# Even steps: the 128-wide rest of the slot is issued after the step's half bulk operation

## The chip, the core and the metric

One core of a Trainium2 chip runs the whole program. The metric is the device time of one execution in microseconds (us), the median of several runs. One execution was also recorded by the hardware profiler.

## What is computed

The input x is 8 sequences of 2048 tokens with 512 features, in fp32. Cut to what matters:

```python
xn = layernorm(x)
x_norm = layernorm(xn, g, b); x_norm += conv3(x_norm)            # depthwise, 3 taps
gate, input_gate = split(x_norm @ gate_w.T + gate_b)
Bm = x_norm * sigmoid(input_gate) @ B_w.T + B_b                  # 64 wide
Cm = x_norm @ C_w.T + C_b
def step(state, (b_t, c_t)):                                     # 2048 of these, in sequence
    s = layernorm(state @ A_bar + b_t, g_st, b_st)
    return s, c_t * s
s = (scan(step) @ D_w.T + D_b) * sigmoid(gate)
out = x + s * silu(xn @ W.T + b + (xn @ V_r) @ C.T)
```

The scan is the only part that is sequential over time. Its state is 8 sequences by 64 numbers.

## The kernel before

The 2048 tokens are cut into 32 chunks (NC) of 64 tokens (CT). All engines run the same loop over chunks, called `iteration(i, ...)`. In iteration i the scan (part F) goes through chunk i, while the dense work of part A prepares chunk i+1 and that of part C finishes chunk i-1. Nothing is planned by a compiler: for every engine the constants at the head of the file (V_CONV, V_YS, V_SG, V_XG, V_ADD, V_G for VectorE, PE_... for TensorE) say behind which scan step t (0 to 63) each piece of dense work is put. Every engine works through its own queue in order, and semaphores join them.

**The scan.** Each token t has a slot of 194 numbers in the tile `dw` for each of the 8 sequences: column CR holds the factor r, CE a constant, CD:CM (64 wide) the centred state w before it is scaled, CM:CM2 (64 wide) and CM2:SLOT (64 wide) what the next two tokens take from it. Steps come in pairs.

- An even step (`even_step`) on VectorE: L947 forms w from the slot before, multiplied by the factor r of the step before. It waits for r (`r_ready`) and for the slot (`a_ready`). L934 (`square_sum`) squares and sums w into q; a second instruction, DVE_READ_ACCUMULATOR, writes q out and raises `q_ready`. L951 then updates the last 128 columns of the slot (CM:SLOT) from a product in the PSUM bank `scanP`; it waits for that product (`p_ready`) and raises `rest_ready`. Below, L951 is called "the rest".
- GpSimd (POOL, L428) turns q into r = q^-0.5 and raises `r_ready`.
- An odd step (`odd_step`): L961 forms w. It waits for `r_ready` and for `rest_ready`, as it reads what the rest wrote. Then L934 again, L964 transposes w for TensorE (`wT_ready`), and L969 updates 64 columns (`a_ready`).
- TensorE (`look_ahead`, L1309 and L1310) multiplies the transposed w of an odd step by the matrices of two tokens ahead, and raises `p_ready` for the next even step's rest.

**The bulk operations.** After the scan's instructions of a step, the loop of VectorE's `iteration` puts at most one piece of dense work in a full chunk: half a tile, 256 columns wide. They are L832 and L839 (the conv taps), L852 (`gated_x`), L862 (`gated_silu`), L874 (`state_times_c`), L887 (`gated_ssm`) and L898 (`add_x`); the last chunk has L907, L917 and L929 as well. A bulk operation comes in two halves; in a full chunk the first half stands at an odd step and the second at an even step, and only the first half waits for another engine. In a full chunk 25 of the 32 even steps hold one: 8 conv taps, 1 of L874 and 4 each of L852, L862, L887 and L898. The last chunk (31) has no conv taps and no L852.

So before the change the queue of VectorE at an even step with bulk work is L947, L934, L951, bulk, and then L961 of the odd step.

Of the kernel before, what the change touches and what calls it, by code (L numbers as in the profile page):

```python
# [15 lines left out]
B = 8  # L16
# [5 lines left out]
CT = 64  # L22
# [12 lines left out]
CR, CE, CD, CM, CM2, SLOT = 0, 1, 2, 2 + S, 2 + 2 * S, 2 + 3 * S  # L35
# [81 lines left out]
def build(nc, x, ident_d, gateT_d, WT_d, VT_d, CrT_d, BT_d, CwT_d, DT_d, vec_d, small_d, Bb_d, out):  # L117
    with ExitStack() as ctx:
        def sb(name, shape, dt=F32):
            return ctx.enter_context(nc.sbuf_tensor(name, shape, dt))  # L120
# [47 lines left out]
        dw = sb("dw", [32, CT, SLOT])  # L168
# [70 lines left out]
        def wait_for(eng, name, per, n, k):  # L239

            v = n * per + k
            if isinstance(v, int) and v <= 0:
                return
            eng.wait_ge(s[name], v)
# [533 lines left out]
        def _(dve):  # L778
# [46 lines left out]
            def left_tap(c, k, h):  # L825
                if h == 0:
                    wait_for(dve, "t1_done", KH, c, k + 1)
                if k == 0 and h == 0:
                    wait_for(dve, "halo_y", 1, c, 1)
                rows = slice(B // 2 * h, B // 2 * (h + 1))  # L830
                bank = cbank[k][:, TH * h:TH * (h + 1)].rearrange("p (b t) -> p b t", b=B // 2)
                V.scalar_tensor_tensor(out=bank, in0=y[:, k, rows, 0:CT], scalar=v_("conv_w0", k), in1=bank,  # L832
                                       op0=ALU.mult, op1=ALU.add).then_inc(s["conv_half"], 1)

            def right_tap(c, k, h, p):
                wait_for(dve, "conv_half", 2 * KH, c, 2 * k + h + 1)
                rows = slice(B // 2 * h, B // 2 * (h + 1))
                bank = cbank[k][:, TH * h:TH * (h + 1)].rearrange("p (b t) -> p b t", b=B // 2)
                ins = V.scalar_tensor_tensor(out=xnorm[p][:, k, TH * h:TH * (h + 1)].rearrange("p (b t) -> p b t", b=B // 2),  # L839
                                             in0=y[:, k, rows, 2:CT + 2], scalar=v_("conv_w2", k), in1=bank,  # L840
                                             op0=ALU.mult, op1=ALU.add)
                if h:
                    ins.then_inc(s["xnorm_done"], 1)

            def gated_x(c, m, h, p):
                if h == 0:
                    wait_for(dve, "igs_done", KH, c, m + 1)
                if m == 0 and h == 0:
                    wait_for(dve, "b_mm", 1, c, 0)
                    wait_for(dve, "xnorm_done", KH, c, KH)  # L850
                part = slice(TH * h, TH * (h + 1))
                ins = V.scalar_tensor_tensor(out=xg[:, m, part], in0=(mbank["ig", m] if c else ibank[m])[:, part], scalar=1.0,  # L852
                                             in1=xnorm[p][:, m, part], op0=ALU.add, op1=ALU.mult)
                if h:
                    ins.then_inc(s["xg_done"], 1)

            def gated_silu(c, m, h, p):
                if h == 0:
                    wait_for(dve, "gates_done", KH, c, m + 1)
                    wait_for(dve, "silu_done", KH, c, m + 1)  # L860
                part = slice(TH * h, TH * (h + 1))
                ins = V.scalar_tensor_tensor(out=G[p][:, m, part], in0=mbank["gate", m][:, part], scalar=1.0,  # L862
                                             in1=G[p][:, m, part], op0=ALU.add, op1=ALU.mult)
                if h:
                    ins.then_inc(s["g_done"], 1)

            def state_times_c(c, h, p):
                if h == 0:
                    wait_for(dve, "sn_done", 1, c, 1)
                    wait_for(dve, "cT_done", 1, c, 1)  # L870
                    wait_for(dve, "ssm_mm", KH, c, 0)
                rows = slice(B // 2 * h, B // 2 * (h + 1))
                by_time = lambda a: a.rearrange("p (b q t) -> p b q t", b=B, q=NQ)[:, rows]
                ins = V.tensor_tensor(by_time(ys[0:S, :]),  # L874
                                      tbank["wr", 0][0:S, :].rearrange("p (q b t) -> p b q t", b=B, q=NQ)[:, rows],
                                      by_time(cT[p][:]), ALU.mult)
                if h:
                    ins.then_inc(s["ys_done"], 1)
# [43 lines left out]
            def last_sum(q, h):  # L922
                if h == 0:
                    wait_for(dve, "last_o", 1, q, 1)
                    if q == 0:
                        dve.wait_ge(s["last_x"], 16 * NQ)
                        wait_for(dve, "xfill", KH, LAST, KH)
                part = slice(HH * h, HH * (h + 1))
                V.tensor_tensor(z[:, q, part], last_o[q][:, part], xa[:, q, part], ALU.add).then_inc(s["last_add"], 1)  # L929

            def square_sum(i, t):
                wait_for(dve, "w_ready", CT, i, t + 1)
                w_eps = dw[0:B, t, CE:CD + S]
                V.scalar_tensor_tensor(out=wq[:], in0=w_eps, scalar=1.0 / S, in1=w_eps, op0=ALU.mult, op1=ALU.mult,  # L934
                                       accum_out=q[:]).then_inc(s["q_ready"], 1)

            def even_step(i, t):

                before = (t - 1) % CT
                r = dw[0:B, before, CR:CR + 1]  # L940
                if i == 0 and t < DIRECT:
                    dve.wait_ge(s["dfirst_done"], t // 2 + 1)
                if i == 0 and t == DIRECT:
                    wait_for(dve, D_IN[0], 16, i, 16)
                wait_for(dve, "r_ready", CT, i, t)
                wait_for(dve, "a_ready", PAIRS, i, t // 2)
                V.scalar_tensor_tensor(out=dw[0:B, t, CD:CM], in0=dw[0:B, before, CM:CM2], scalar=r,  # L947
                                       in1=dw[0:B, t, CD:CM], op0=ALU.mult, op1=ALU.add).then_inc(s["w_ready"], 1)
                square_sum(i, t)
                wait_for(dve, "p_ready", PAIRS, i, t // 2 + 1)  # L950
                V.scalar_tensor_tensor(out=dw[0:B, t, CM:SLOT], in0=scanP[0:B, 0:2 * S], scalar=r,  # L951
                                       in1=dw[0:B, t, CM:SLOT], op0=ALU.mult, op1=ALU.add
                                       ).then_inc(s["rest_ready"], 1)
# [164 lines left out]
            def iteration(i, p, parts):  # L1118
                A, F, C = ("A" in parts), ("F" in parts), ("C" in parts)
                gate_at = V_G if A else V_G_LAST  # L1120
                conv_at = V_CONV if i else V_CONV_FIRST
                xg_at = V_XG if i else V_XG_FIRST
                for t in range(CT):
                    if F:
                        (odd_step if t % 2 else even_step)(i, t)
                    if A:
                        if t in conv_at:
                            k, part = divmod(conv_at.index(t), 4)
                            if part < 2:
                                left_tap(i + 1, k, part)  # L1130
                            else:
                                right_tap(i + 1, k, part - 2, 1 - p)
                        if t in xg_at:
                            gated_x(i + 1, *divmod(xg_at.index(t), 2), 1 - p)
                    if F:
                        if t in gate_at:
                            gated_silu(i, *divmod(gate_at.index(t), 2), p)
                    if C:
                        if t in V_YS:
                            state_times_c(i - 1, V_YS.index(t), 1 - p)  # L1140
                        if t in V_SG:
                            gated_ssm(i - 1, *divmod(V_SG.index(t), 2), 1 - p)
                        if t in V_ADD:
                            add_x(i - 1, *divmod(V_ADD.index(t), 2))
                    if i == LAST:
                        if t in V_YS_LAST:
                            last_states(V_YS_LAST.index(t))
                        if t in V_SG_LAST:
                            last_gated(*divmod(V_SG_LAST.index(t), 2))
                        if t in V_ADD_LAST:  # L1150
                            last_sum(*divmod(V_ADD_LAST.index(t), 2))

            iteration(0, 0, "ASF")
            iteration(1, 1, "ASFC")
# [386 lines left out]
```

## Time and profile before

| | us |
|---|---|
| median of 3 runs | 2497.48 |
| lowest and highest | 2494.24, 2498.33 |
| the profiled execution's own time | 2498.52 |
| its span, first to last instruction | 2496.7 |
| TensorE (PE) busy | 2455.1 |
| VectorE (DVE) busy | 2187.8 |
| GpSimd (POOL) busy | 1239.9 |
| ScalarE (ACT) busy | 1013.1 |
| mean granted TensorE clock, share of full speed | 0.99 |

Busy time adds up an engine's instructions. It doesn't tell whether the end of the program waits for that engine. For that one reads, in a stretch of some steps, which instruction starts as soon as which other ends. In the listing of instructions by time, the columns are start in us, duration in us, engine, line, operation, tiles written and read, and in brackets the idle time of the engine before it with what ended it. VectorE instructions overlap slightly: the next may start before the bar of the last has ended.

### The profile page before, as it was taken

What the parts mean: (1) busy time and instruction counts of PE and PEld (TensorE: products, weight loads), DVE (VectorE), ACT (ScalarE), POOL (GpSimd) and SP (SyncE); (2) the same over time, 40 slices, a digit from 0 to 9 for tenths busy, and PEclk for the clock granted to TensorE, in tenths of its full rate; (3) what the DMA queues carried; (4) which work ended last, traced back from release to release, by engine and by line L of the source; (5) the groups of instructions that cost most, each with busy time, mean ns of one, the idle gap of its engine ahead of it and who ended that gap; (6) DMA issues with size and microseconds to landing.
All of it is one profiled execution on the core that took longest, in us unless ns stands there. A gap on an engine that the chain in (4) does not pass through costs nothing.

```text
span 2496.7 us, 42418 instructions
## 1 busy us (share of the span) xinstructions
PE 2455.1 (98%) x10031; PEld 1313.3 (53%) x10031; DVE 2187.8 (88%) x10934; ACT 1013.1 (41%) x1859; POOL 1239.9 (50%) x2433
## 2 busy tenths in 40 slices
PE   8999999999999999999999999999999999999996
PEld 4555555555555555555555555555555555555544
DVE  5788889988889988899988899888899888899886
ACT  4444433444434443434443434443334444344310
POOL 1445555545555545555445555445555455555443
PEclk9999999999999999999999999999999999999997
DMA  3112212122112122112122112122112122111121
GB/s 112 24 43 59 51 39 53 48 52 60 45 39 58 49 51 60 43 41 55 47 55 60 43 41 55 48 55 60 42 41 52 49 58 59 39 44 52 31 59 36
DMA packets 99542, 125.14 MB, mean 50 GB/s; under 512 B 31967, under 2 KB 48479, under 8 KB 99296
## 3 DMA queue, kind: packets, MB, share of 16 engines
q1 hardware_dynamic: 98560, 121.25, 19.7%
q8 instruction: 85, 1.39, 0.2%
q10 hardware_dynamic: 736, 1.18, 0.2%
q14 instruction: 161, 1.32, 0.2%
HBM read 71.96 MB, written 33.55 MB: 42 GB/s over the span
## 4 chain that ended last, share of the span: by engine, by line
PE 43%; POOL 28%; DVE 20%; issue 8%; ACT 0%; DMA 0%; SPq 0%; POOLq 0%; DVEq 0%; ACTq 0%
POOL dw L428 25%; PE bank L1243 9%; DVE wq L934 8%; PE bank L1232 7%; PE bank L1222 7%; DVE dw L961 6%; DVE dw L947 5%; PE bank L1309 5%; PE bank L1310 4%; POOL ln L455 3%; PE bank L1253 2%; PE bank L1271 2%; PE bank L1262 2%; PE bank L1182 1%; PE bank L1198 1%
## 5 line engine op out<-in xcount | busy, mean ns | idle before, releaser
L428 POOL TENSOR_TENSOR dw<-q,minus_half 8x1 f32<-8x1 f32 x2048 | 1085.7, 530 | 1190.4 <-DVE wq L934 1157.4
L1309 PEld LDWEIGHTS bank<-Mscan,wT 128*65 128x65 f32 x2046 | 228.0, 136 | 618.1 <-issue 607.0
L1232 PE MATMUL bank<-xnorm,gateT 128*128 128x512 f32 x1024 | 507.5, 594 | 0.9 <-DVE sgT L887 0.9
L934 DVE SCALAR_TENSOR_TENSOR wq<-dw 8x65 f32<-8x65 f32 x2048 | 443.2, 216 | 70.2
L1243 PE MATMUL bank<-xnorm,gateT 128*128 128x512 f32 x1024 | 503.3, 597 | 0.0
L1222 PE MATMUL bank<-xnT,WT 128*128 128x512 f32 x1024 | 494.5, 593 | 0.0
L1309 PE MATMUL bank<-Mscan,wT 128*65 128x128 f32 x2046 | 404.4, 279 | 14.0 <-DVE wT L964 11.8
L1310 PE MATMUL bank<-Mscan,wT 128*65 128x128 f32 x2046 | 392.4, 274 | 0.0
L961 DVE SCALAR_TENSOR_TENSOR dw<-dw 8x64 f32<-8x64 f32 x1024 | 279.3, 273 | 111.4 <-POOL dw L428 85.7
L951 DVE SCALAR_TENSOR_TENSOR dw<-bank,dw 8x128 f32<-8x128 f32 x1024 | 342.7, 335 | 12.8 <-PE bank L1310 10.4
L947 DVE SCALAR_TENSOR_TENSOR dw<-dw 8x64 f32<-8x64 f32 x1024 | 279.4, 273 | 77.4 <-POOL dw L428 75.6
L1310 PEld LDWEIGHTS bank<-Mscan,wT 128*65 128x65 f32 x2046 | 253.9, 138 | 0.2
L584 ACT ACTIVATE bank<-bank,vec 128x512 f32<-128x512 f32 x128 | 84.7, 662 | 397.2 <-PE bank L1243 397.2
L969 DVE SCALAR_TENSOR_TENSOR dw<-dw 8x64 f32<-8x64 f32 x1024 | 244.4, 239 | 0.0
L964 DVE STREAM_TRANSPOSE wT<-dw 32x64 f32<-32x64 f32 x1024 | 232.9, 227 | 0.0
L1222 PEld LDWEIGHTS bank<-xnT,WT 128*128 128x128 f32 x1024 | 167.1, 191 | 93.9 <-issue 93.9
L1243 PEld LDWEIGHTS bank<-xnorm,gateT 128*128 128x128 f32 x1024 | 163.4, 192 | 93.6 <-issue 91.9
L640 ACT ACTIVATE bank<-bank,vec 128x512 f32<-128x512 f32 x128 | 84.7, 662 | 299.4 <-PE bank L1232 299.4
L1232 PEld LDWEIGHTS bank<-xnorm,gateT 128*128 128x128 f32 x1024 | 169.0, 191 | 57.9 <-issue 56.8
L636 ACT ACTIVATE G<-bank,vec 128x512 f32<-128x512 f32 x128 | 87.4, 683 | 197.1 <-PE bank L1222 193.4
L934 DVE DVE_READ_ACCUMULATOR wq<-dw 8x1 f32 x2048 | 144.8, 71 | 0.0
L1198 PE MATMUL bank<-ident,sgT 128*128 128x128 f32 x496 | 135.1, 273 | 0.0
(188 smaller groups left out, 2746.0 us busy)
## 6 DMA issues: line engine op xcount, KB each, us to landing
xc<-in_x SPq DMA_DIRECT2D x252, 128.0 KB, 2.8
xa<-in_x SPq DMA_DIRECT2D x252, 128.0 KB, 2.7
out<-o SPq DMA_DIRECT2D x248, 128.0 KB, 2.4
dw<-dtok SPq DMA_DIRECT2D x127, 96.0 KB
wtok<-dw SPq DMA_DIRECT2D x128, 33.0 KB
gateT<-in_gateT SPq DMA_DIRECT2D x1, 2048.0 KB
WT<-in_WT SPq DMA_DIRECT2D x1, 1024.0 KB, 7.6
xa<-in_x SPq DMA_DIRECT2D x4, 256.0 KB
```

The costliest lines, as they stand in the source:

```text
L428: nc.gpsimd.tensor_tensor(dw[0:B, t, CR:CR + 1], q[:], minus_half[0:B, 0:1], ALU.pow).then_inc(s["r_ready"], 1)
L934: V.scalar_tensor_tensor(out=wq[:], in0=w_eps, scalar=1.0 / S, in1=w_eps, op0=ALU.mult, op1=ALU.mult, accum_out=q[:]).then_inc(s["q_ready" ...
L947: V.scalar_tensor_tensor(out=dw[0:B, t, CD:CM], in0=dw[0:B, before, CM:CM2], scalar=r, in1=dw[0:B, t, CD:CM], op0=ALU.mult, op1=ALU.add).t ...
L951: V.scalar_tensor_tensor(out=dw[0:B, t, CM:SLOT], in0=scanP[0:B, 0:2 * S], scalar=r, in1=dw[0:B, t, CM:SLOT], op0=ALU.mult, op1=ALU.add).t ...
L961: V.scalar_tensor_tensor(out=dw[0:B, t, CD:CM], in0=dw[0:B, before, CM:CM2], scalar=r, in1=dw[0:B, t, CD:CM], op0=ALU.mult, op1=ALU.add).t ...
L964: V.transpose(wT[0:32, 0:S], dw[:, t, CD:CM]).then_inc(s["wT_ready"], 1)
L969: V.scalar_tensor_tensor(out=dw[0:B, t, CM:CM2], in0=dw[0:B, before, CM2:SLOT], scalar=r, in1=dw[0:B, t, CM:CM2], op0=ALU.mult, op1=ALU.ad ...
L1222: ins = mm(mbank["ffn", m][:], WT[:, k, P * m:P * m + P], xnT[:, k, :], start=(k == 0), stop=(k == KH - 1))
L1232: ins = mm(mbank["gate", m][:], gateT[:, k, P * m:P * m + P], xnorm[p][:, k, :], start=(k == 0), stop=(k == KH - 1))
L1243: ins = mm((mbank["ig", m] if c else ibank[m])[:], gateT[:, k, H + P * m:H + P * m + P], xnorm[p][:, k, :], start=(k == 0), stop=(k == KH ...
L1309: mm(scanP[0:WIDE, 0:2 * S], wT[:, 0:WIDE], Mscan[:, 0, :], start=True, stop=False)
L1310: mm(scanP[0:WIDE, 0:2 * S], wT[:, 32:32 + WIDE], Mscan[:, 1, :], start=False, stop=True).then_inc(s["p_ready"], 1)
```

## The change

The last third of `even_step` becomes a function of its own, `even_rest`, and the loop calls it at the end of an even step, behind whatever bulk work that step holds. Steps without bulk work keep their order. No instruction is added or removed, and every wait stays with its instruction.

```diff
                 square_sum(i, t)
+
+            def even_rest(i, t):
+
+                r = dw[0:B, (t - 1) % CT, CR:CR + 1]
                 wait_for(dve, "p_ready", PAIRS, i, t // 2 + 1)
                 V.scalar_tensor_tensor(out=dw[0:B, t, CM:SLOT], in0=scanP[0:B, 0:2 * S], scalar=r,
                                        in1=dw[0:B, t, CM:SLOT], op0=ALU.mult, op1=ALU.add
@@
                         if t in V_ADD_LAST:
                             last_sum(*divmod(V_ADD_LAST.index(t), 2))
+                    if F and t % 2 == 0:
+                        even_rest(i, t)
```

## Rows read from the trace of the kernel before

**Rows 1.** The page: engines busy, and the chain that ended last

```profile
PE 2455.1 (98%) x10031; PEld 1313.3 (53%) x10031; DVE 2187.8 (88%) x10934; ACT 1013.1 (41%) x1859; POOL 1239.9 (50%) x2433
...
PE 43%; POOL 28%; DVE 20%; issue 8%; ACT 0%; DMA 0%; SPq 0%; POOLq 0%; DVEq 0%; ACTq 0%
```

**Rows 2.** Instructions by time, all engines: an even conv step, then an odd one

```profile
1203.78 0.27 DVE L947 SCALAR_TENSOR_TENSOR dw<-dw 8x64 f32<-8x64 f32 x1
...
1204.09 0.22 DVE L934 SCALAR_TENSOR_TENSOR wq<-dw 8x65 f32<-8x65 f32 x1
1204.24 0.07 DVE L934 DVE_READ_ACCUMULATOR wq<-dw 8x1 f32 x1
1204.24 0.34 DVE L951 SCALAR_TENSOR_TENSOR dw<-bank,dw 8x128 f32<-8x128 f32 x1
...
1204.39 0.53 POOL L428 TENSOR_TENSOR dw<-q,minus_half 8x1 f32<-8x1 f32 x1 [0.64 <-DVE wq L934]
1204.50 0.47 DVE L832 SCALAR_TENSOR_TENSOR bank<-y,vec,bank 128x256 f32<-128x256 f32 x1
...
1204.95 0.27 DVE L961 SCALAR_TENSOR_TENSOR dw<-dw 8x64 f32<-8x64 f32 x1
```

**Rows 3.** VectorE by time: an even step whose rest is late, with bulk work

```profile
92.02 0.07 DVE L934 DVE_READ_ACCUMULATOR wq<-dw 8x1 f32 x1
92.57 0.34 DVE L951 SCALAR_TENSOR_TENSOR dw<-bank,dw 8x128 f32<-8x128 f32 x1 [0.47 <-PE bank L1310]
92.83 0.46 DVE L839 SCALAR_TENSOR_TENSOR xnorm<-y,vec,bank 128x256 f32<-128x256 f32 x1
93.22 0.27 DVE L961 SCALAR_TENSOR_TENSOR dw<-dw 8x64 f32<-8x64 f32 x1
```

**Rows 4.** VectorE by time: step 48 of chunk 15

```profile
1255.98 0.07 DVE L934 DVE_READ_ACCUMULATOR wq<-dw 8x1 f32 x1
1256.12 0.34 DVE L951 SCALAR_TENSOR_TENSOR dw<-bank,dw 8x128 f32<-8x128 f32 x1
1256.38 0.40 DVE L898 TENSOR_TENSOR o<-bank,xc 128x256 f32<-128x256 f32 x1
1256.71 0.26 DVE L961 SCALAR_TENSOR_TENSOR dw<-dw 8x64 f32<-8x64 f32 x1
```

**Rows 5.** VectorE by time: an even step whose rest is late, without bulk work

```profile
77.31 0.34 DVE L951 SCALAR_TENSOR_TENSOR dw<-bank,dw 8x128 f32<-8x128 f32 x1 [0.40 <-PE bank L1310]
77.75 0.27 DVE L961 SCALAR_TENSOR_TENSOR dw<-dw 8x64 f32<-8x64 f32 x1
```

**Rows 6.** VectorE by time: another such step, in the last chunk

```profile
2443.35 0.34 DVE L951 SCALAR_TENSOR_TENSOR dw<-bank,dw 8x128 f32<-8x128 f32 x1 [1.30 <-PE bank L1310]
2443.80 0.27 DVE L961 SCALAR_TENSOR_TENSOR dw<-dw 8x64 f32<-8x64 f32 x1
```

**Rows 7.** One line's instructions, durations in ns (least/median/most): L951 and VectorE's separate waits

```profile
L951 DVE SCALAR_TENSOR_TENSOR dw<-bank,dw x1024: 333/334/341, 63.7 to 2480.7; 8x128 f32<-8x128 f32 x171
...
L244 DVEq EVENT_SEMAPHORE  x2433: 21/21/499, 5.9 to 2481.1; - x188
```

**Rows 8.** VectorE's instructions by line: count, busy us, mean ns, idle before

```profile
L832 DVE SCALAR_TENSOR_TENSOR bank<-y,vec,bank 128x256 f32<-128x256 f32 x256 | 119.7, 469 | 0.4 <-ACT bank L573 0.3
L839 DVE SCALAR_TENSOR_TENSOR xnorm<-y,vec,bank 128x256 f32<-128x256 f32 x256 | 117.4, 460 | 0.0
L862 DVE SCALAR_TENSOR_TENSOR G<-bank,G 128x256 f32<-128x256 f32 x256 | 103.2, 403 | 0.0
L887 DVE TENSOR_TENSOR sgT<-bank,G 128x256 f32<-128x256 f32 x248 | 99.9, 403 | 0.0
```

**Rows 9.** VectorE's waits: total us, times, longest us

```profile
DVE dw L961 <- POOL dw L428: 85.7, 234, 0.5
...
DVE dw L951 <- PE bank L1310: 10.4, 14, 3.7
```

**Rows 10.** The chain that ended last between 1200 and 1220 us: shares by line

```profile
by line: POOL dw L428 48.6%; DVE wq L934 18.9%; DVE dw L961 12.8%; DVE dw L947 11.2%; issue 11.0%
```

## The prediction

> **What bounds the kernel now.** I read the page first [rows 1]. It offers two readings: TensorE is busy for 98% of the span and holds 43% of the chain that ended last, while VectorE and GpSimd are less busy. A bar that is nearly full is no proof. The chain follows back one route through instructions that touch each other, and where TensorE always has something to do it can follow TensorE's queue as well. So next I read single steps by time, to see which start comes right behind which end.
>
> At an even step [rows 2], w starts at 1203.78. The square sum starts at 1204.09 and hands q over at 1204.24, when the accumulator is read. GpSimd starts at 1204.39 and takes 0.53, so r is there at 1204.92. L961, the next step's w, starts at 1204.95, 0.03 later. One step is thus 1.17 us, and 2048 of them are some 2400 of the span's 2497 us. The chain of a quiet stretch is this loop and nothing else [rows 10]. The rest's wait for TensorE's product costs 10.4 us in 14 long waits over the whole run [rows 9]. So **the recurrence is the bound**, not TensorE, and what counts is the interval from the accumulator read to the next w. It is 1204.95 - 1204.24 = 0.71 us. Whatever VectorE has to do between those two points is free as long as it fits in 0.71.
>
> Before the change it fits: the rest starts at 1204.24, the bulk operation at 1204.50 (0.26 later), and 0.45 is left for it [rows 2].
>
> **The change part by part.** Nothing is added or removed. In 7 of 32 even steps of a full chunk no bulk work stands between, and the order stays. In the others the rest and the bulk operation swap places, and three things have to be priced.
>
> 1. How soon may VectorE start something behind a bulk operation? Rows in which VectorE itself was late show it, as there nothing else holds the next start. Behind a conv tap it is 93.22 - 92.83 = 0.39 [rows 3], behind the others 1256.71 - 1256.38 = 0.33 [rows 4]. The lines fall into these two classes by duration, 460 to 469 ns and 403 ns [rows 8]. I take it that the rest, which waits only for an early product, starts as promptly as L961 did.
>
> 2. How long is it from the start of the rest to the start of L961 if nothing is between them? Before the change that is normally hidden: the bulk operation covers the rest's tail. But a few rests came late with nothing behind them, and long after r was there. They give 77.75 - 77.31 = 0.44 [rows 5] and 2443.80 - 2443.35 = 0.45 [rows 6]; one at 69.89 gives 0.44 too. The rest lasts 0.34 in these rows, so **the handoff costs 0.10 behind the rest's end**. It is dearer than the one from w to the square sum, which is 1204.09 - (1203.78 + 0.27) = 0.04 [rows 2]. The reason I see is that L961 waits for two semaphores, and one of them sits in a sequencer instruction of its own, an EVENT_SEMAPHORE of 21 ns, in front of L961 [rows 7]; in the rows read, the wait for the rest is the one set apart. The change doesn't touch the waits, so I take 0.10. With the rest's median of 334 ns [rows 7] that is 0.434 from the start of the rest to L961.
>
> 3. Which steps? Conv taps at even steps: 8 in each of chunks 0 to 30, so 248. Others: L852 and L862 4 each in 31 chunks, plus 4 of L862 in the last chunk, and 9 of L874, L887 and L898 in each of chunks 1 to 31, so 124 + 124 + 4 + 279 = 531.
>
> The sum, against the 0.71 that the loop allows:
> - conv: 0.39 + 0.434 = 0.824, so 0.114 late; 248 x 0.114 = 28.3 us
> - others: 0.33 + 0.434 = 0.764, so 0.054 late; 531 x 0.054 = 28.7 us
>
> Together +57.0 us. All of it lies on the recurrence: nothing catches it up, because the odd step, its square sum and GpSimd stand behind L961. An odd step with bulk work is unchanged. Queued behind the later rest are L961 and the whole odd step with its transpose, so TensorE gets its input later by the same amount, but its fixed work per pair then has more room.
>
> Against it stands what the swap covers. Where the product is late, the bulk operation now runs in the wait.
> - Step 48 of some 28 chunks has the rest 0.14 late [rows 4]. Before, the interval is 1256.71 - 1255.98 = 0.73; after, it is 0.764 whether the product comes at 0 or at 0.33. The loss is 0.034 and not 0.054: 28 x 0.02 = 0.6 back.
> - Three steps of chunk 0 wait about 0.5 to 1 us with a conv tap behind. Before 93.22 - 92.02 = 1.20 [rows 3]; after 0.55 + 0.434 = 0.98. That is 0.22 gained where 0.114 lost was counted: 1.0 back for the three.
> - In the last chunk TensorE's queue sets the pace in several stretches (a wait of 1.30 us, [rows 6]). A shift of VectorE is absorbed there or won by the cover. I count its 21 steps at nothing: 1.1 back.
>
> 57.0 - 0.6 - 1.0 - 1.1 = +54.3 us. The profiled execution took 2498.5 us and would take 2552.8. It is 1.0 above the median of the three runs, so against 2497.5 I forecast **2551.8 us, 2.2% slower**.
>
> **A rule against this.** The rows show that the square sum starts 0.04 behind the end of the w on which it waits, while an instruction without such a wait starts 0.08 before the end of the one in front (the bulk at 1204.50, the rest's end at 1204.58) [rows 2]. The Trainium skill, in "VectorE: DVE Perf Modes", section "The DRAIN you can't avoid", says that every VectorE instruction empties the pipe before the next starts, and that a semaphore between two of them costs nothing extra. By that rule a dependent pair costs the same as any pair, rest and bulk could be swapped for nothing, and the time would be that of the second rival below. The rows here disagree by 0.12 for an ordinary wait and by 0.18 for L961's.
>
> **The rivals.**
>
> The handoff is 0.04, not 0.10. If the wait for the rest ends up on L961 itself once the rest is the later of the two, the price is that of w to square sum. Conv: 0.39 + 0.334 + 0.04 = 0.764, 0.054 late, 248 times, 13.4 us. Others: 0.704, on time. With some 2 us back that is +11, so 2508.5. Against it are rows 5 and 6: there too the rest came last, and the price was 0.10. Chance 0.09.
>
> The dependence costs nothing. Then the swapped pair needs 0.33 + 0.26 = 0.59 or 0.39 + 0.26 = 0.65, both under 0.71, and only the covered waits change: 28 x 0.02 + 3 x 0.28 = 1.4 us off, and something in the last chunk, so some 2495.5. Every row with a wait speaks against it. Chance 0.05.
>
> Faster: TensorE's product is the bound more often than I think, as the 43% of the page suggest. The place is the rest's wait for `p_ready`; the swap hides up to 0.39 of each wait. Twenty-eight steps of 0.14 (of which 0.07 can be idle), three of chunk 0 and some ten in the last chunk give at most 28 x 0.07 + 3 x 0.39 + 10 x 0.33 = 6.4 us, so 2491.1. All waits together are 10.4 [rows 9], which caps it. It decides only if the handoff costs nothing and the last chunk gives nothing back to TensorE. Chance 0.03.
>
> More than forecast: if the rest starts some 0.02 later behind a bulk operation than L961 did, or takes its longest, 341 ns [rows 7], 779 steps lose up to 0.027 more, 21 us, giving some 2573. I see no row for the first part. Chance 0.08, and its lower half is inside my range.
>
> **How the numbers follow.** The forecast has 0.75, the small handoff 0.09, no cost 0.05, faster 0.03, more 0.08. The range of the forecast alone takes the rounding of its terms to 0.01 us: 779 x 0.01 = 8 us either way, plus 2 for the last chunk, 2541 to 2562. For 8 in 10 it reaches into the dearer case: 2540 to 2566. A measurement of this kernel can tell about 0.2%, 5 us, from no change. Slower by more: 0.75 + 0.09 + 0.08 = 0.92. Within: the free case, 0.05. Faster: 0.03.
>
> **What the profile after would show.** At an even conv step L951 starts 0.39 behind the conv tap, and L961 0.43 to 0.44 behind L951; the interval from accumulator read to L961 is 0.82 to 0.83, and 0.76 to 0.77 with the other bulk lines. Even steps without bulk work and all odd steps keep 1.17. GpSimd's idle time grows by the added time, and L961's idle time is put down to L951. Step 48 is no longer than its neighbours. I am wrong if L961 starts within 0.05 of the rest's end (the small handoff), if it starts 0.03 behind GpSimd's end with bulk work at the step (no cost), or if L951 starts clearly later than 0.39 or 0.33 behind the bulk operation.

## The result, and the profile after

The changed kernel takes 2558.7 us in the median of 4 runs (2555.2 to 2560.9) against 2496.9 before (the median of 4 runs here, one more than in the table above): ratio 1.025, 95% interval 1.0238 to 1.0262. It is slower by 61.8 us; 54.3 were forecast, and the range of 2540 to 2566 holds the time. The profiled execution took 2555.2 us with a span of 2553.4, so 56.7 more than the profiled one before (both by time and by span).

The page after, in its parts on busy time and on the chain that ended last, answers to [rows 1]:

```profile
PE 2480.9 (97%) x10031; PEld 1289.4 (50%) x10031; DVE 2189.5 (86%) x10934; ACT 1015.7 (40%) x1859; POOL 1239.9 (49%) x2433
...
DVE 47%; POOL 34%; issue 13%; PE 4%; DVEq 1%; DMA 0%; POOLq 0%; SPq 0%; ACT 0%
```

VectorE and GpSimd do what they did before (2189.5 and 1239.9 us busy against 2187.8 and 1239.9). For these two all added time is time in which they wait. TensorE's bar grows by 25.8 us (from 2455.1) with the same 10031 matmuls, and its share of the chain falls from 43% to 4%: here the chain follows the loop nearly everywhere. DVEq, VectorE's sequencer, goes from 0% to 1%. How little the share of the chain says by itself is told below, under the last experiment.

The lines changed place: the rest is L955 now (L951 before), the odd step's w is L965 (L961 before). Instructions by time, an even conv step after, which answers to [rows 2]:

```profile
1230.04 0.22 DVE L934 SCALAR_TENSOR_TENSOR wq<-dw 8x65 f32<-8x65 f32 x1
1230.19 0.07 DVE L934 DVE_READ_ACCUMULATOR wq<-dw 8x1 f32 x1
1230.19 0.47 DVE L832 SCALAR_TENSOR_TENSOR bank<-y,vec,bank 128x256 f32<-128x256 f32 x1
1230.34 0.53 POOL L428 TENSOR_TENSOR dw<-q,minus_half 8x1 f32<-8x1 f32 x1 [0.64 <-DVE wq L934]
1230.58 0.33 DVE L955 SCALAR_TENSOR_TENSOR dw<-bank,dw 8x128 f32<-8x128 f32 x1
1231.02 0.27 DVE L965 SCALAR_TENSOR_TENSOR dw<-dw 8x64 f32<-8x64 f32 x1
```

GpSimd ends at 1230.87, as early behind the accumulator read as before (0.68). But L965 starts only at 1231.02: 0.39 from the conv tap to the rest, 0.44 from the rest to L965, together 0.83 instead of 0.71. An even step with L887, after:

```profile
1259.55 0.07 DVE L934 DVE_READ_ACCUMULATOR wq<-dw 8x1 f32 x1
1259.55 0.41 DVE L887 TENSOR_TENSOR sgT<-bank,G 128x256 f32<-128x256 f32 x1
1259.89 0.33 DVE L955 SCALAR_TENSOR_TENSOR dw<-bank,dw 8x128 f32<-8x128 f32 x1
1260.32 0.27 DVE L965 SCALAR_TENSOR_TENSOR dw<-dw 8x64 f32<-8x64 f32 x1
```

Here it is 0.34 + 0.43 = 0.77. VectorE's waits after, which answer to [rows 9]:

```profile
DVE dw L965 <- POOL dw L428: 91.1, 240, 0.5
...
DVE dw L955 <- PE bank L1316: 4.3, 5, 2.8
...
DVE dw L965 <- DVE dw L955: 1.4, 3, 0.5
```

The rest's wait for TensorE falls from 10.4 us to 4.3. The loss itself hardly shows in this view: the 0.10 behind the rest is listed in 3 places alone, and not, as I had forecast, as a wait of L965 for L955 at every step. The page's groups show it better. The odd step's w and GpSimd's r before, with the idle time behind the second bar:

```profile
L428 POOL TENSOR_TENSOR dw<-q,minus_half 8x1 f32<-8x1 f32 x2048 | 1085.7, 530 | 1190.4 <-DVE wq L934 1157.4
...
L961 DVE SCALAR_TENSOR_TENSOR dw<-dw 8x64 f32<-8x64 f32 x1024 | 279.3, 273 | 111.4 <-POOL dw L428 85.7 <-DVE dw L951 0.5
```

and after:

```profile
L428 POOL TENSOR_TENSOR dw<-q,minus_half 8x1 f32<-8x1 f32 x2048 | 1085.7, 530 | 1250.1 <-DVE wq L934 1233.3
...
L965 DVE SCALAR_TENSOR_TENSOR dw<-dw 8x64 f32<-8x64 f32 x1024 | 279.1, 273 | 176.6 <-POOL dw L428 91.1
```

GpSimd is idle for 59.7 us more in front of r, and VectorE for 65.2 us more in front of the odd step's w, of which it puts 5.4 down to GpSimd. For the remainder it names no releaser.

Read over all steps of both traces, from the accumulator read to the next w (medians, in us):

| even steps | number | before | forecast | after |
|---|---|---|---|---|
| no bulk work | 237 | 0.712 | 0.712 | 0.713 |
| conv taps L832, L839 | 248 | 0.712 | 0.824 | 0.831 |
| L874, L887, L898 | 279 | 0.712 to 0.717 | 0.764 | 0.770 to 0.771 |
| L852, L862 | 252 | 0.713 | 0.764 | 0.781 |

These are 1016 of the 1024 even steps; the other 8 hold L907, L917 or L929 of the last chunk. From the first w to the last the scan is 59.1 us longer, 58.5 of it at even steps and 0.6 at odd ones. A full chunk of 64 steps is 2.0 to 2.3 us longer.

### The profile page after: what moved, and what is told of

It reads as the page before. It is cut to its first block, busy times and chain, and to the rows that moved or that the text cites. A ratio compares the mean times of both kernels' runs of the same rounds, so it can differ in the third digit from the quotient of the medians.

```text
span 2553.4 us, 42418 instructions
## 1 busy us (share of the span) xinstructions
PE 2480.9 (97%) x10031; PEld 1289.4 (50%) x10031; DVE 2189.5 (86%) x10934; ACT 1015.7 (40%) x1859; POOL 1239.9 (49%) x2433
## 4 chain that ended last, share of the span: by engine, by line
DVE 47%; POOL 34%; issue 13%; PE 4%; DVEq 1%; DMA 0%; POOLq 0%; SPq 0%; ACT 0%
POOL dw L428 29%; DVE wq L934 14%; DVE dw L965 9%; DVE dw L947 9%; DVE dw L955 6%; POOL ln L455 5%; DVE bank L832 2%; DVE xnorm L839 2%; DVE G L862 2%; DVE sgT L887 2%; PE bank L1249 1%; PE bank L1228 1%; DVEq L244 0%; DVE o L898 0%; DVE xg L852 0%
## 5 line engine op out<-in xcount | busy, mean ns | idle before, releaser
L1315 PEld LDWEIGHTS bank<-Mscan,wT 128*65 128x65 f32 x2046 | 207.9, 135 | 710.7 <-issue 708.3
L965 DVE SCALAR_TENSOR_TENSOR dw<-dw 8x64 f32<-8x64 f32 x1024 | 279.1, 273 | 176.6 <-POOL dw L428 91.1
L955 DVE SCALAR_TENSOR_TENSOR dw<-bank,dw 8x128 f32<-8x128 f32 x1024 | 339.5, 332 | 4.3 <-PE bank L1316 4.3
L1316 PEld LDWEIGHTS bank<-Mscan,wT 128*65 128x65 f32 x2046 | 253.1, 138 | 0.2
```

Source lines behind the costliest of these rows:

```text
L1315: mm(scanP[0:WIDE, 0:2 * S], wT[:, 0:WIDE], Mscan[:, 0, :], start=True, stop=False)
L1316: mm(scanP[0:WIDE, 0:2 * S], wT[:, 32:32 + WIDE], Mscan[:, 1, :], start=False, stop=True).then_inc(s["p_ready"], 1)
```

## The experiments

My theory: two things make the loss, both on the recurrence. The rest now begins behind a bulk operation, and the next w begins 0.10 behind the rest's end, where 0.035 would do, because its wait for the rest is the one in a separate sequencer instruction. The rivals: the 0.10 is the price of the rest's result itself; the loss comes from elsewhere and is spread over all steps; TensorE is the bound.

### Which of two waits is the separate one

Both kernels were run with the two waits of the odd step's w exchanged in the code.

```diff
-                wait_for(dve, "r_ready", CT, i, t)
                 wait_for(dve, "rest_ready", PAIRS, i, t // 2 + 1)
+                wait_for(dve, "r_ready", CT, i, t)
```

The order of the kernel before:

> The order of the kernel before; in odd steps alone the two waits of L961 change places in the code, so that the one for the rest sits on the instruction and the one for r in the separate sequencer instruction. My theory: a wait in the separate instruction starts L961 0.10 behind what it waits for, a wait on the instruction 0.035. r comes at 0.68 behind the accumulator read, so L961 starts at 0.78 instead of 0.712 in all 1024 even steps: +0.068 x 1024 = +70 us, some 2567. Rival, the price of 0.10 is that of the rest's own result (a 128-wide write to be read next), whichever way it is waited for: no change, 2497.

Measured: 2567.5 us against 2497.1, ratio 1.0283 (1.0268 to 1.0298). In the order of the kernel before, with waits exchanged, by time:

```profile
1235.65 0.07 DVE L934 DVE_READ_ACCUMULATOR wq<-dw 8x1 f32 x1
1235.65 0.33 DVE L951 SCALAR_TENSOR_TENSOR dw<-bank,dw 8x128 f32<-8x128 f32 x1
1235.80 0.53 POOL L428 TENSOR_TENSOR dw<-q,minus_half 8x1 f32<-8x1 f32 x1 [0.65 <-DVE wq L934]
1235.91 0.47 DVE L832 SCALAR_TENSOR_TENSOR bank<-y,vec,bank 128x256 f32<-128x256 f32 x1
1236.43 0.27 DVE L961 SCALAR_TENSOR_TENSOR dw<-dw 8x64 f32<-8x64 f32 x1
```

GpSimd ends at 1236.33, and L961 starts at 1236.43, 0.10 later, where it was 0.03 in [rows 2]. The median interval from GpSimd's end to L961 is 103 ns against 35, and the even steps are 70.0 us longer in sum, the odd ones 2.0. The one exchange of two lines costs more than the whole change.

The traces also show of what the 0.10 consists. In this run the separate EVENT_SEMAPHORE (L244) waits for r. It starts 38 ns behind GpSimd's end, lasts 21 ns, and L961 starts 45 ns behind its end (medians). In the changed kernel it waits for the rest, and the three pieces behind a conv tap are 39, 21 and 45 ns.

The changed kernel with the same edit:

> The changed kernel with the same swap of the two waits. My theory: the rest's handoff falls from 0.10 to 0.035, the wait for r rises to 0.10. Conv: the rest gives 0.39 + 0.334 + 0.035 = 0.76, r gives 0.78, so 0.78; all other even steps 0.78. So about the same +70 us over before as the kernel before with swapped waits, 2567; and the rest's end to L961 is no longer 0.10 but whatever r leaves. Rival, the price belongs to the rest's result: conv stays at 0.83 and the others at 0.77, as in the changed kernel, 2558.

Measured: 2569.3 us, ratio 1.0289 (1.0274 to 1.0304). The changed order with waits exchanged, VectorE by time:

```profile
1240.60 0.07 DVE L934 DVE_READ_ACCUMULATOR wq<-dw 8x1 f32 x1
1240.60 0.47 DVE L832 SCALAR_TENSOR_TENSOR bank<-y,vec,bank 128x256 f32<-128x256 f32 x1
1240.99 0.33 DVE L955 SCALAR_TENSOR_TENSOR dw<-bank,dw 8x128 f32<-8x128 f32 x1
1241.38 0.27 DVE L965 SCALAR_TENSOR_TENSOR dw<-dw 8x64 f32<-8x64 f32 x1
```

L965 starts 0.06 behind the rest's end (1241.32); if the rest's result itself cost 0.10, it could not. This kernel has 2569.3 where 2567 was expected, and not the rival's 2558. Conv steps fall to 0.783, below the 0.831 of the changed kernel, while every other even step rises to 0.78 or 0.79. With the waits in this order the rest no longer ends the wait; r does. The price belongs to the separate wait.

### One wait in the changed kernel

The rest and GpSimd's r now raise the same semaphore, so that the odd step's w waits for one count.

```diff
-                wait_for(dve, "r_ready", CT, i, t)
-                wait_for(dve, "rest_ready", PAIRS, i, t // 2 + 1)
+                wait_for(dve, "r_ready", 1, 0, (3 * (i * CT + t) + 1) // 2)
...
-                                       ).then_inc(s["rest_ready"], 1)
+                                       ).then_inc(s["r_ready"], 1)
```

The other waits for that semaphore count 3 for 2 steps in the same way.

> The changed kernel, but the rest and GpSimd's r raise one and the same semaphore, so L961 has a single wait, on the instruction. My theory: handoff 0.035 for both. Conv 0.39 + 0.333 + 0.035 = 0.76, 0.05 late, 248 times, +12 us; others 0.336 + 0.330 + 0.035 = 0.70, hidden behind r at 0.712, nothing; some 2 us back: about +10 over before, 2507. Rival, the price belongs to the rest's result: no change against the changed kernel, +60.

Measured: 2505.2 us against 2497.1, ratio 1.003 (1.0017 to 1.0042), so +8 over before. The changed order with one semaphore, VectorE by time, first a conv step, then one with L887:

```profile
1209.49 0.07 DVE L934 DVE_READ_ACCUMULATOR wq<-dw 8x1 f32 x1
1209.49 0.47 DVE L832 SCALAR_TENSOR_TENSOR bank<-y,vec,bank 128x256 f32<-128x256 f32 x1
...
1209.88 0.33 DVE L955 SCALAR_TENSOR_TENSOR dw<-bank,dw 8x128 f32<-8x128 f32 x1
1210.25 0.27 DVE L964 SCALAR_TENSOR_TENSOR dw<-dw 8x64 f32<-8x64 f32 x1
...
1231.04 0.07 DVE L934 DVE_READ_ACCUMULATOR wq<-dw 8x1 f32 x1
1231.04 0.41 DVE L887 TENSOR_TENSOR sgT<-bank,G 128x256 f32<-128x256 f32 x1
1231.38 0.33 DVE L955 SCALAR_TENSOR_TENSOR dw<-bank,dw 8x128 f32<-8x128 f32 x1
1231.75 0.27 DVE L964 SCALAR_TENSOR_TENSOR dw<-dw 8x64 f32<-8x64 f32 x1
```

The handoff is 0.04 (1209.88 + 0.33 to 1210.25). The conv step needs 0.76, and the step with L887 0.71: the rest is done at 0.67, and r sets the start again. By the medians that is 0.762 in 248 steps and 0.712 to 0.713 in all others. So of the change's 62 us some 54 were the separate wait and 8 the place of the rest itself. The 8 are what is left of 248 x 0.050 = 12.4 us at conv steps; in this trace the last chunk is 3.5 us shorter than before, and part of that is chance, as told below.

### The change in halves

The rest goes behind the bulk operation at conv steps alone, or at the others alone.

```diff
                 square_sum(i, t)
+                if not swapped(i, t):
+                    even_rest(i, t)
+
+            def swapped(i, t):
+                return t in (V_CONV if i else V_CONV_FIRST) and i < LAST
...
-                    if F and t % 2 == 0:
+                    if F and t % 2 == 0 and swapped(i, t):
```

> The rest goes behind the bulk operation only where that is a conv tap (248 steps); everywhere else the order of before. My theory: 248 x (0.831 - 0.712) = +29.5 us, less 1 for the late products of chunk 0: +28.5, 2525. Rival, that the loss comes from elsewhere than these intervals (GpSimd or TensorE late everywhere): not in the proportion of these steps; by their share of the swapped steps, 248 of 779, it would be +19.

Measured: 2523.7 us against 2497.1, ratio 1.0108 (1.0093 to 1.0123), +26.6 where 28.5 was expected and the rival had 19. Conv steps have 0.831, all others of full chunks 0.712 to 0.718.

> The complement of the kernel that swaps at conv steps alone: the rest goes behind the bulk operation in the 531 even steps whose bulk operation is not a conv tap; conv steps keep the order of before. My theory: the medians of the changed kernel are 0.781 for L852 and L862 (252 steps) and 0.771 for L874, L887 and L898 (279 steps) against 0.712: 17.4 + 16.5 = +33.9 us, less 3 for late products: +31, 2528. With the conv-only kernel's +26.6 this should add up to the changed kernel's gap of 58 to 62. Rival, that the two parts share a cost (one slow step makes the next one slow): the two together give clearly more than the whole.

Measured: 2529.6 us against 2495.2, ratio 1.0138 (1.0124 to 1.0152), +34.3 where 31 was expected. The two halves give 26.6 + 34.3 = 60.9, the whole 61.8; in the traces the scan is 27.2 and 31.7 us longer, together 58.9, the whole 59.1. The loss is a plain sum of single steps; within what can be measured none makes its neighbour slow.

### TensorE with less work

Two of the four partial products of the gate projection are left out in the kernel before, so the gate is computed from half of the features.

```diff
             def gate(c, m, k, p, i, middle):
+                if k in (1, 2):
+                    return
```

> The kernel before without the matmuls k = 1 and k = 2 of the gate projection: 256 of TensorE's matmuls of 128x512 are left out, so the gate is computed from half of the features. My theory, the recurrence is the bound: TensorE loses 256 x 0.43 = 110 us of work, the time loses 1 to 4 us (step 48's late product, and stretches of the last chunk, where the gate's matmuls set the pace and some 3 us may go). Rival, TensorE is the bound for the 43% of the span that the page's chain gives it: some 0.43 x 110 = 47 us off, 2450.

Measured: 2496.0 us against 2495.2, ratio 1.0003 (0.9993 to 1.0012). The page with half of the gate, busy time:

```profile
PE 2283.6 (91%) x9519; PEld 1204.4 (48%) x9519; DVE 2186.9 (88%) x10934; ACT 1013.1 (41%) x1859; POOL 1240.0 (50%) x2433
```

The 256 matmuls of the code are 512 of the profile's, and the 110 us that I had counted for them was too low: TensorE lost 171.5 us of busy time (2455.1 before). The rival's 43% of that would be 74 us, and the time didn't move. In the trace step 48 is 28 ns shorter in the mean, and the last chunk 1.1 us, too little to measure. TensorE isn't the bound, whatever share of the chain the page gives it.

### Only the cover, and only the semaphore

What is left of the idea is to run bulk work in the wait for a late product. This kernel has one semaphore and swaps only where the product was late: steps 10, 20 and 24 of chunk 0, step 48 of chunks 1 to 30, nine steps of the last chunk.

> The rest goes behind the bulk operation only where TensorE's product is late (chunk 0: steps 10, 20, 24; step 48 of chunks 1 to 30; nine steps of the last chunk), and the one shared semaphore gives L961 a single wait; everywhere else the order of before. My theory: only the cover is left: chunk 0 3 x 0.28 = 0.8, step 48 0.7, last chunk up to 2.5: -2 to -4 us, 2493 to 2495. Rival, TensorE is the bound more often: over 6 us off, under 2491. Rival, the last chunk's gain is given back to TensorE's queue: -1.5.

Measured, in 11 runs: 2494.6 us against 2495.2, ratio 0.9999 (0.999 to 1.0007). No gain that can be measured, where I expected 2 to 4 us. The single steps do what was expected: step 48 is 28 ns shorter in the mean. Chunks 0 and 31 are 2.3 and 3.3 us shorter in this trace, but much of that (1.8 us at step 2 of chunk 0, 1.1 at step 32 of chunk 31) lies at steps that were not edited for it. The chunks between are 0.1 longer each, although their step 48 is shorter; why stayed open.

The order of the kernel before with one semaphore:

> The order of the kernel before, but the rest and GpSimd's r raise the same semaphore, so L961 has one wait. My theory: no change, 2497 within 2, as r is the later of the two and its wait was on the instruction already; the semaphore helps only where the rest comes last. Rival, a separate sequencer instruction costs VectorE's queue time at every odd step even where its wait is long over: up to 1024 x 0.021 = 21 us off.

Measured: 2495.5 us against 2495.2, ratio 1.0004 (0.9995 to 1.0013). A separate sequencer wait whose time is long over costs nothing. Of the cases tried, it costs where it is the last to be fulfilled.

This run's page also shows what the share of the chain is worth:

```profile
PE 94%; DVE 3%; POOL 2%; issue 1%; DMA 0%; SPq 0%; ACT 0%; POOLq 0%; DVEq 0%
```

TensorE has 94% of the chain here, 43% in [rows 1] and 4% in the kernel that swaps at late steps alone, and the three take the same time (ratios 1.0004 and 0.9999 to the kernel before). No kernel tried here beats the kernel before.

## Why the prediction was right, point by point

**The bound.** Right. The recurrence sets the time: 58.5 of the 59.1 us by which the scan grew lie at even steps, and 171.5 us less of TensorE's work change nothing.

**When VectorE is free behind a bulk operation.** Forecast 0.39 and 0.33 from rows in which VectorE was late; the trace after has medians of 0.394 and 0.336. The 0.004 to 0.006 come with bulk operations that last 6 to 7 ns longer right behind the accumulator read: at even steps the medians are 407 ns against 401 for the shorter lines, and 465 to 473 against 458 to 467 for the conv taps.

**From the rest to the next w.** Forecast 0.434 from three late rests; after a conv tap it is 0.437, after L874, L887 and L898 0.434, after L852 and L862 0.445. The handoff alone is 0.104 to 0.105, and 0.115 behind the last two. That the separate wait is the cause was argued in the prediction and is shown by the exchanged waits and by the single semaphore.

**Counts and sum.** 248 and 531 steps as forecast. With the measured intervals the sum is 248 x 0.119 + 279 x 0.059 + 252 x 0.068 = 29.5 + 16.5 + 17.1 = 63.1 us where I had 57.0. So each step was sized 0.005 to 0.014 too low; this is the term that was off. More than half of the 6.1 us is at L852 and L862.

**What the cover gives back.** Forecast 2.7, and one part of that is a slip: it takes back 1.1 us for 21 steps of the last chunk, but the sum holds only 13 of them (9 of L874, L887 and L898, 4 of L862; the 8 with L907, L917 and L929 were never counted), so 0.7 was right and the forecast should have been 54.7. By the trace 63.1 - 59.1 = 4.0 came back. Two parts came as forecast. The three late steps of chunk 0 (10, 20 and 24) gave back 1.0. Step 48 costs 34 ns in the median (forecast 0.034; the mean is 39). The rest is largely chance. At step 2 of chunk 0 and step 32 of the last chunk, which hold no bulk work and so kept their order, the trace after is 0.9 and 1.1 us shorter. The last chunk as a whole is 2.1 us shorter, but it is also 1.6 us shorter in the trace of the conv steps alone, where nothing in it was edited. So a gain in the last chunk isn't shown.

**From the scan to the whole.** 59.1 of the scan became 56.7 of the span because the first w came at 60.87 instead of 63.26. That part is before the scan and not touched by the change; in the traces of the experiments it lies between 59.8 and 65.7. The medians, which differ by 61.8 (59 to 65 by the interval), don't depend on one such draw. So the forecast of 54.3 was low by some 5 to 8 us: 6.1 by the size of the steps, less 1.3 that came back beyond the forecast; the draws of the single executions make up the difference between 59.1 and 61.8.

**The rivals.** The small handoff, 0.04, gave 2508.5. It isn't what the change does, but it is what one semaphore makes of it: 2505.2. The rule that a dependent pair costs nothing extra is refuted. An instruction without a wait starts 0.07 before the end of the rest in front of it (the bulk operations before the change), and the odd step's w 0.036 behind that end with the wait on it and 0.105 with the separate one. The section of the Trainium skill that the prediction names for that rule, "The DRAIN you can't avoid" in "VectorE: DVE Perf Modes", also says: "A next op that is not held starts earlier". The prediction left that out, and the 0.07 agrees with it; its finding that the semaphore costs nothing extra is of 8 copies and doesn't hold for these small instructions. The faster case fails twice: its place, the wait for the product, is worth less than can be measured, even without the cost of the swap.

## What to carry to other kernels

Where a loop is bound by a chain over two engines, an instruction of that chain's own data may be free only because something stands between it and its reader; look at what follows it before you move it to the end. Of an instruction that waits for two semaphores only one wait sits on the instruction, in this program the one written first; the other costs 0.07 us more when it ends last, so put the later one first, or let both raise one semaphore. A nearly full bar and a large share of the chain didn't make TensorE the bound. What told was to read, step by step, which start comes right behind which end.

## What the runs showed of the hardware beyond that

The handoff behind the separate wait is 0.104 to 0.105 with five of the lines of bulk work in front of the rest, and 0.115 with L852 and L862 (252 steps, some 2.5 us in all). Both are SCALAR_TENSOR_TENSOR operations with a constant scalar; the conv taps, of the same operation with a scalar from a tile, have 0.105. The 10 ns lie between the end of the EVENT_SEMAPHORE and the start of w, which is 55 ns instead of 45. They don't belong to the rest's result: in the changed order with waits exchanged, where the separate wait is for r, L965 starts 0.114 behind GpSimd's end at these steps and 0.103 or 0.104 at the others. In the order of the kernel before with waits exchanged, where the bulk operation stands behind the rest, all lines have 0.103 to 0.104. So the difference needs the rest behind one of these two lines, and a separate wait that ends last. With one semaphore it can't be seen, since r ends the wait there. Why it arises stayed open; no run was made for it.
